# Cross attention of a decoder kernel: the convolution kernel's products turned round, four channels in four column groups

## The reference, cut to what matters

```python
dt = jnp.exp(log_dt)
A = A_re + 1j * A_im
C = C_re + 1j * C_im
dtA = dt[:, None] * A
dC = C * (jnp.exp(dtA) - 1.0) / A
powers = jnp.exp(dtA[:, :, None] * jnp.arange(L))
K = 2.0 * jnp.einsum('dn,dnl->dl', dC, powers).real   # 128 channels, 64 states, L = 1024
```

## Time and profile before

| | |
|---|---|
| three runs, median (lowest to highest) | 1830.77 us (1829.9 to 1832.34) |
| the profiled execution's own time | 1832.86 us |
| its span in the profile | 1831.1 us |
| PE busy, share of the span | 1457.1 us, 80% |
| DVE busy | 1319.4 us, 72% |
| ACT busy | 923.9 us, 50% |
| POOL busy | 691.3 us, 38% |
| the second stage of the cross attention | about 296 to 512 us of the span |
| mean granted clock of PE | 0.882 of full speed |

### The profile page before, as it was taken

The page is one execution under the profiler, slowest core; times in us unless marked ns, Lnnn a source line. Parts: engine busy times, 40 slices in busy tenths (PEclk is TensorE's granted clock), DMA queues, the critical chain, the costliest instruction groups (busy, mean ns, idle before and its releaser), DMA issues. The chain is left out here.

```text
span 1831.1 us, 19912 instructions
## 1 busy us (share of the span) xinstructions
PE 1457.1 (80%) x6613; PEld 791.4 (43%) x6669; DVE 1319.4 (72%) x3065; ACT 923.9 (50%) x1447; POOL 691.3 (38%) x524
## 2 busy tenths in 40 slices
PE   5776999899985467887888878888857538999798
PEld 2223444355543312544555545555545324333365
DVE  5998568655156479899989999999857465767433
ACT  4654213656312204786777778777831104666321
POOL 0764212122000003888788888878820020000012
PEclk8899999999977768899899999989887757999899
DMA  5000110000057100000000000000020030000000
GB/s 138 1 1 3 46 58 16 0 1 1 0 126 144 47 14 1 1 1 1 1 1 1 1 1 1 1 1 1 1 83 11 15 78 1 1 1 1 1 0 12
DMA packets 30685, 37.21 MB, mean 20 GB/s; under 512 B 13859, under 2 KB 23812, under 8 KB 29448
## 3 DMA queue, kind: packets, MB, share of 16 engines
q1 hardware_dynamic: 29028, 24.03, 4.8%
q10 hardware_dynamic: 1544, 11.79, 3.2%
HBM read 29.57 MB, written 6.24 MB: 20 GB/s over the span
## 5 line engine op out<-in xcount | busy, mean ns | idle before, releaser
L1461 PE MATMUL psum<-film_ka,film_context_qa 97*128 97x512 bf16 (+1 forms) x832 | 343.2, 414 | 143.8 <-DVE search_and_weigh_kept L1656 63.6
L1833 ACT ACTIVATE search_and_weigh_e<-psum,search_and_weigh_bias 128x512 f32<-128x512 f32 (+1 forms) x416 | 267.9, 666 | 110.2 <-PE psum L1463 105.4
L1656 DVE MAX8 search_and_weigh_kept<-psum 128x8 f32<-128x171 f32 (+2 forms) x1216 | 317.3, 323 | 5.0 <-PE psum L1463 3.8
L1463 PE MATMUL psum<-film_kb,film_context_qb 128*128 128x512 bf16 (+1 forms) x777 | 319.1, 411 | 0.0
L1682 DVE SCALAR_TENSOR_TENSOR search_and_weigh_e<-psum,film_context_top,search_and_weigh_e 128x512 f32<-128x512 f32 (+1 forms) x283 | 200.8, 717 | 36.8 <-ACT search_and_weigh_e L1833 34.6
L1704 POOL TENSOR_TENSOR search_and_weigh_e<-search_and_weigh_e,search_and_weigh_keep 128x512 f32<-128x512 f32 (+1 forms) x133 | 150.4, 1131 | 167.3 <-ACT search_and_weigh_keep L1812 163.3
L1461 PEld LDWEIGHTS psum<-film_ka,film_context_qa 97*128 97x128 bf16 x832 | 92.2, 111 | 250.2 <-DVE search_and_weigh_e L1682 95.7
L1738 PEld LDWEIGHTS psum<-ctx_rows,search_and_weigh_mean_T 128*128 128x128 f32 (+1 forms) x816 | 132.3, 208 | 32.8 <-issue 6.0
L1708 POOL TENSOR_TENSOR search_and_weigh_mean<-search_and_weigh_e 128x512 f32<-128x512 f32 (+1 forms) x104 | 133.9, 1288 | 12.7 <-DVE search_and_weigh_e L1682 5.6
L1713 POOL TENSOR_TENSOR search_and_weigh_mean<-search_and_weigh_mean,search_and_weigh_e 128x512 f32<-128x512 f32 (+1 forms) x104 | 127.7, 1227 | 8.2
L1738 PE MATMUL psum<-ctx_rows,search_and_weigh_mean_T 128*128 128x96 f32 (+1 forms) x816 | 129.0, 284 | 0.9
(11 more groups left out here) (547 smaller groups left out, 2687.5 us busy)
## 6 DMA issues: line engine op xcount, KB each, us to landing
film_kb<-film_k_rows ACTq DMA_DIRECT2D x4, 1601.0 KB
film_ka<-film_k_rows ACTq DMA_DIRECT2D x3, 1601.0 KB
ctx_T<-in_ctx_T SPq DMA_DIRECT2D x1, 2401.5 KB
gqa_experts_w<-in_L_ffn_W SPq DMA_DIRECT2D x1, 2048.0 KB
film_convolve_back<-in_dft_back SPq DMA_DIRECT2D x1, 1728.0 KB, 12.9
film_k_rows<-cross_attention_film_hi SPq DMA_DIRECT2D x6, 256.0 KB, 2.0
film_k_rows<-cross_attention_film_mid SPq DMA_DIRECT2D x6, 256.0 KB, 2.0
film_k_rows<-cross_attention_film_low SPq DMA_DIRECT2D x6, 256.0 KB, 2.0
```

The source lines that it names most:

```text
L1461: pe.matmul(out, a["qa"][0:ROWS, h, rows], a["ka"][0:ROWS, h, c + b:c + b + cols], start=True, stop=False)
L1463: last = pe.matmul(out, a["qb"][:, h, rows], a["kb"][:, h, c + b:c + b + cols], start=False, stop=True)
L1656: last = dve.max(kept[:, h % 2, first + s, :], bank[:, lo:hi])
L1833: act.activation(e[:, n % RING, sub, 0:PIECES[u][1]], ps[:, SEARCH_BANKS + q % WEIGH_BANKS, 0:PIECES[u][1]], ACT.Exp, bias=bias[:, i % 2, ...
```

## The change

The products are turned round: `left[:, d, :]` (8 columns) is now the weights, and the 128 columns of powers move. Four channels stand in the four column groups of PE and write partitions 0 to 7, 32 to 39, 64 to 71 and 96 to 103 of one bank; 16 channels (two groups q) fill bank 4. DVE zeroes that bank once. For each of the eight rounds r, ACT copies bank 4 to `rows` in SBUF, PE turns it with four transposes of 128x128 into bank 5, and ACT copies the useful columns to `k_tok`. The places in the written orders are: PE's products as before; ACT's `s4d_copy_rows(r)` at k = 20 + 4 r, behind the S4D step of that k and ahead of its exponentials; PE's `s4d_turn(r)` at k = 21 + 4 r, behind the products; ACT's `s4d_copy_kernel(r)` at k = 22 + 4 r. The large copy at the end goes. No transfer is added or removed.

```diff
+PER_BANK = 2 * GROUP
...
-def s4d_vector(dve, link, k):
+def s4d_vector(dve, link, k, bank):
 
     sem = k["sem"]
+    dve.memset(bank, 0.0).then_inc(sem["zeroed"], 1)
...
         if q >= RING_Q:
-            dve.wait_ge(sem["k_psum"], q - RING_Q + 1)
+            dve.wait_ge(sem["k_rows"], q - RING_Q + 1)
...
-    dve.wait_ge(sem["k_ready"], 1)
+    dve.wait_ge(sem["k_ready"], D // PER_BANK)
...
-def s4d_copy(act, k, banks):
-    act.wait_ge(k["sem"]["k_psum"], NG)
-    act.activation(k["k_tok"][:], banks.rearrange("p b (d j) -> p j (b d)", j=NT),
-                   ACT.Copy).then_inc(k["sem"]["k_ready"], 1)
+def s4d_copy_rows(act, k, bank, r):
+    sem = k["sem"]
+    act.wait_ge(sem["k_rows"], 2 * (r + 1))
+    if r >= 1:
+        act.wait_ge(sem["k_psum"], r)
+    act.activation(k["rows"][:], bank, ACT.Copy).then_inc(sem["rows_copied"], 1)
+
+
+def s4d_copy_kernel(act, k, bank, r):
+
+    sem = k["sem"]
+    act.wait_ge(sem["k_psum"], r + 1)
+    act.activation(k["k_tok"][:, :, r * PER_BANK:(r + 1) * PER_BANK],
+                   bank.rearrange("p (n x) -> p x n", x=32)[:, 0:NT, :], ACT.Copy).then_inc(sem["k_ready"], 1)
+
+
+def s4d_tensor(pe, k, bank, q):
 
     sem = k["sem"]
     if q == 0:
         pe.wait_ge(sem["left_ready"], 1)
+        pe.wait_ge(sem["zeroed"], 1)
+    if q >= 2 and q % 2 == 0:
+        pe.wait_ge(sem["rows_copied"], q // 2)
     pe.wait_ge(sem["powers"], q + 1)
     for c in range(GROUP):
         d = q * GROUP + c
-        last = pe.matmul(banks[:, d // 64, (d % 64) * NT:(d % 64 + 1) * NT], k["i_angle"][:, q % RING_Q, c, :],
-                         k["left"][:, d, :], start=True, stop=True)
+        slot = d % PER_BANK // 4
+        last = pe.matmul(bank[32 * (c % 4):32 * (c % 4) + NT, slot * P:(slot + 1) * P], k["left"][:, d, :],
+                         k["i_angle"][:, q % RING_Q, c, :], start=True, stop=True,
+                         tile_position=(0, 32 * (c % 4)))
+    last.then_inc(sem["k_rows"], 1)
+
+
+def s4d_turn(pe, k, bank, r):
+    sem = k["sem"]
+    pe.wait_ge(sem["rows_copied"], r + 1)
+    if r >= 1:
+        pe.wait_ge(sem["k_ready"], r)
+    for slot in range(4):
+        last = pe.transpose(bank[:, slot * P:(slot + 1) * P], k["rows"][:, slot * P:(slot + 1) * P],
+                            k["ident"][:])
     last.then_inc(sem["k_psum"], 1)
...
+S4D_ROWS_AT = S4D_PE_AT + S4D_PE_EVERY + 1
...
+    s4d_rows = {S4D_ROWS_AT + 2 * S4D_PE_EVERY * r: r for r in range(D // PER_BANK)}
...
                 if k in s4d_products:
-                    s4d_tensor(pe, s4d, s4d_banks, s4d_products[k])
+                    s4d_tensor(pe, s4d, ps[:, 4, :], s4d_products[k])
+                if k - 1 in s4d_rows:
+                    s4d_turn(pe, s4d, ps[:, 5, :], s4d_rows[k - 1])
...
                 if k in s4d_steps:
                     s4d_scalar(act, s4d, s4d_steps[k])
+                if k in s4d_rows:
+                    s4d_copy_rows(act, s4d, ps[:, 4, :], s4d_rows[k])
+                if k - 2 in s4d_rows:
+                    s4d_copy_kernel(act, s4d, ps[:, 5, :], s4d_rows[k - 2])
...
-            s4d_copy(act, s4d, s4d_banks)
```

More of the change, by code:

```diff
@@ L516, in s4d_buffers @@
     k["d_skip"] = m.sb("s4d_d_skip", [1, D])
+    k["rows"] = m.sb("s4d_rows", [P, HALF])
+    k["ident"] = g["ident"]
     k["sem"] = {n: m.sem(f"s4d_{n}") for n in (
         "loaded", "dt_ready", "parts_ready", "small_ready", "small_done", "j_ready", "j_done",
-        "left_ready", "i_ready", "sin_done", "grown", "decayed", "powers", "k_psum", "k_ready")}
+        "left_ready", "i_ready", "sin_done", "grown", "decayed", "powers", "zeroed", "k_rows", "rows_copied",
+        "k_psum", "k_ready")}
     k["k_tok"] = g["k_tok"]
@@ L677, in s4d_scalar @@
             act.activation(decay, decay, ACT.Exp).then_inc(sem["decayed"], 1)
-def s4d_copy(act, k, banks):
-    act.wait_ge(k["sem"]["k_psum"], NG)
-    act.activation(k["k_tok"][:], banks.rearrange("p b (d j) -> p j (b d)", j=NT),
-                   ACT.Copy).then_inc(k["sem"]["k_ready"], 1)
-def s4d_tensor(pe, k, banks, q):
+def s4d_copy_rows(act, k, bank, r):
[10 more added lines that the diff above has]
+def s4d_tensor(pe, k, bank, q):
     sem = k["sem"]
@@ L875, in cross_attention @@
     key_units = {KEYS_FIRST + KEYS_EVERY * u: u for u in range(len(UNITS))}
-    s4d_banks = ps[:, 4:6, :]
     s4d_steps = dict(zip(S4D_AT, range(1, S4D_STEPS)))
     s4d_products = {S4D_PE_AT + S4D_PE_EVERY * q: q for q in range(NG)}
+    s4d_rows = {S4D_ROWS_AT + 2 * S4D_PE_EVERY * r: r for r in range(D // PER_BANK)}
     def chunk_cols(c):
@@ L930, in _ @@
             dve.tensor_scalar(minus_top[:, :, DC], top[:], -1.0, None, ALU.mult).then_inc(top_ready, 1)
-            s4d_vector(dve, link, s4d)
+            s4d_vector(dve, link, s4d, ps[:, 4, :])
             dve.wait_ge(pv_done, KT)
```

## The result

The changed kernel took 1835.91 us (median of 7 runs, 1833.22 to 1842.16) beside 1830.77 us for the kernel before, a ratio of 1.0039 with a 95% interval of 1.0020 to 1.0058. It is slower, as forecast, and inside the range, but by 5.1 us where the prediction said 15.5. The number is that of rival A (+4.9 us, the clock holds), so it has to be seen whether its mechanism is too. Two later comparisons on other occasions gave 1.0039 (1.0019 to 1.0059) and 1.0042 (1.0026 to 1.0059). The profiled execution took 1835.33 us, span 1833.5.

What follows compares the result with a forecast made beforehand. PE was taken to bound the S4D stretch. Products (-27.2 + 8.8), turns (+4.0), stalls (+19.4), iteration 17 (+1.3), old waits (-1.2) and clock (+10.6) gave +15.7 us, +15.4 by period; forecast 1846.3 us, range 1834 to 1856.

Steps and rivals of the forecast that it cites:

- rival A: PE's stalls come but the clock holds, so they cost only their length: +4.9 us, 1835.7 us; chance 0.09.
- The bound: From 361.5 to 496 us PE is busy for the whole 134.5 us and sets the pace of the S4D products.
- the products: PE's 16 S4D groups fall from 1.70 to 0.55 us each: 27.2 us removed, 8.8 us added.
- the turns: 32 added PE transposes in eight rounds of four, 0.5 us a round: +4.0 us on PE's path.
- the copies: ACT's copy of rows takes 0.59 us, its kernel copy about 0.27 us; the latter is covered and costs nothing.
- Rival C: Column groups do not overlap on PE, products take 1.72 us a group: +17.5 us more, 1863.8 us; chance 0.05.
- The six stalls: PE's products at k = 21 to 41 wait 3.24 us each for ACT's row copy behind its S4D block: +19.4 us.
- Rival B: ACT's row copy is in time, PE waits only 1.4 us six times for exponentials: -5.8 us, 1825.0 us; chance 0.06.
- Iteration 17: Shorter first products only make PE wait longer for the exponentials of 16: +1.3 us, no clock cost taken.
- The clock: PE's granted clock falls behind each of six standstills, costing 1.77 us each: +10.6 us.
- the old waits: PE's seven old waits of 0.17 us for late exponentials before the weighted sums go: -1.2 us.
- The sum: All terms give +15.7 us, a check by period +15.4; the whole kernel's median 1830.8 + 15.5 = 1846.3 us.

Runs made afterwards that it cites:

- the padded one: Changed kernel plus 44 dummy one-column PE products at the head of cross attention, moving later code one packet further: 1846.06 us, ratio 1.0069 to the kernel before.
- the last: Changed kernel, nothing edited, measured again on the same chip and beside the same runs of the kernel before: 1840.48 us, ratio 1.0042.
- the first repeat: Changed kernel, nothing edited, measured once more: 1836.74 us beside 1830.48 for the kernel before, ratio 1.0039.
- the last two kernels: Changed kernel with copy, turns and kernel copy one iteration earlier and ACT's block split: 1808.07 us; kernel before with that split alone: 1823.88 us.

## Why the prediction was right or wrong

*The bound, the products, the turns, the copies*: right. 0.55 us forecast and measured for a group; turns 0.56 for 0.5; copies 0.58 and 0.27 for 0.59 and 0.27. Rival C is out.

*The six stalls*: right. 3.24 us forecast, 3.07 in the records; the copy behind ACT's block is the cause, as exchanging the two calls shows. Rival B's stage, built that way, is 5.6 us shorter than before for the 5.8 it had.

*Iteration 17*: 1.0 us of waiting, no fall of the clock: right within 0.3 us.

*The clock*: right, 1.68 us for 1.77 in the typical trace. The forecast took it as certain each time; it isn't. Behind the six stalls it fell six times in three traces (the first, the padded one, the last), and five times in that of the first repeat, where it also held behind the two standstills before the products: 23 of 24 stalls. Rival A is out, though the measured time is its time: the clock did fall, and what made up for it lies elsewhere.

*VectorE, the zeroing, the old waits*: right; periods of 20.47 us for 20.53 leave less than 0.1 us each for a hidden term.

*The sum*: this is the step that failed: "+15.4" for the stage was made "1830.8 + 15.5" for the kernel, which takes everything behind the stage to be as it was. I costed only engines and queues that the diff touches, and said of POOL and SP that they get nothing. But the added PE instructions moved the code of all later parts, and one wait for code, 3.3 us in the traces, went. With this taken back, the changed kernel is 1.0069 times the kernel before, +12.6 us of 1830.77 (9.5 to 15.6), or 11.2 us by the medians. The stage itself varies with the clock: it was 236.36, 230.93, 236.38 and 236.44 us in the four traces with the changed products and order, and 221.17, 221.15, 217.73 and 221.19 us in the four with those of before. On average that is 14.7 us, inside the interval. So the forecast of 15.5 was three times the 5.1 measured, although every term of the sum was within about 1 us. Of the 10.4 us between them 5.2 to 5.6 us by the medians (3.3 us of it seen in the trace) are the code's place. The rest can be the spread of the runs; no run shows a further cause, and none rules one out. That the first pair of profiled executions lay only 2.5 us apart was luck: 6.3 us of it was the clock in the convolution.

## What to carry to other kernels

When a copy is added to a busy engine, its place in that engine's order can cost more than its length: behind a block six copies of 0.58 us made PE stand still for 18.4 us here and lose 10 more to the clock; ahead of the block the stage was 20.8 us shorter, with 6.8 us of waits left, and with the block cut in two and the copy an iteration earlier none was left. When an edit adds instructions ahead of a branch on data, part of the difference in time can be the place of the code; pad one of the two kernels with idle instructions before you credit the edit. A variant that does as expected needs this as much as a surprising one: the last two kernels differ by 15.8 us, and the column groups are worth 13.2. And compare the two kernels' starts of all later parts, in more than one execution each, before a difference there is explained.

## What the runs showed of the hardware

- A block entered by a branch on a value just computed came 1.5 us or 4.3 to 4.9 us after it, by how many instructions PE had ahead of it: with 160 more it was the short wait instead of the long one, with 256 more, one 16 KB packet, the long one again.
- Four column groups on f32 data with weights of 8 columns and 128 moving columns: 8 products in 0.55 us, against 1.70 us with the 128 columns of powers loaded as weights and 8 columns moved.
- The same standstill of PE is paid for by the clock in one execution and not in another: the clock fell behind the 3.1 us in 23 of 24 cases, behind the 2.8 us of the earlier trace rows in 11 of 13 traces and behind its 1.8 us in 8 of 11, and never behind the thirteen waits of 1.0 or 1.1 us. In the repeat the stretches of the earlier trace rows read 1.00 against 0.68 and 0.67 (the second standstill ended 1.4 us earlier there):

```profile
327.20:332.50 5.30, 4.94 (x12) 1.00 0.00 0
348.20:353.40 5.20, 5.20 (x14) 1.00 0.00 0
```

- Single executions of one kernel differ by up to 14 us (1829.95 to 1844.01 in 11 runs of the changed kernel), so a trace's sum and a median can't be matched to better than some microseconds.
